# Resident expert weights, and matmuls without a reader in the routing stage of a graph layer

## The chip, the cores and the metric

The kernel runs on one core of one Trainium2 chip. The metric is the device time of one execution in microseconds; the time before is 579.2 us, the median of 3 runs (577.43 to 580.93).

## The reference

One layer on 1250 nodes with 512 features: a layer norm, two graph convolutions (20000 edges) and a linear attention with a two-matrix tail, all added to `x`, then a routed feed-forward on the normed sum. Only the feed-forward matters for the change:

```python
gate_logits = jnp.einsum('bhnd,hde->bhne', xh, gate_weight)      # 1250 tokens x 8 experts
gates = _sinkhorn(gate_logits)                                   # 8 rounds: over tokens, then over experts
vals, idx = jax.lax.top_k(jnp.swapaxes(gates, -1, -2), n // e)   # 156 tokens for each expert
routed = jnp.take_along_axis(xh[:, :, None, :, :], idx[..., None], axis=3)
outputs = jnp.einsum('ebhmi,ehio->ebhmo', routed, expert_w)      # 156x512 @ 512x512, 8 experts
outputs = outputs * gate_values
routed_back = zeros.at[idx].set(outputs)                         # later experts win
x = x + routed_back
```

## The kernel before

Everything is written by hand for each engine, with semaphores between them; each engine's program runs in the order of the code. The 1250 tokens stand as NT = 10 tiles of 125 rows. A float32 matrix product is made of three passes over rounded parts (high by high, low by high, high by low), so a 512x512 product of a tile is 12 matmuls of 512 columns. ScalarE makes the high part of a weight by a copy that rounds (`WEH`), VectorE the low part by a subtraction from the raw weight (`WEL`, `RAW_E`).

The last third of the program, around the change, has three stages.

*Collect.* For each tile `i` TensorE makes the second graph aggregation in 20 matmuls (L789 to L801), VectorE adds it to `X`, makes the norm statistics, and `Y` is the normed tile. SyncE's queue stores `X` to the output and to a DRAM scratch, and `Y` to the scratch (`store_x`, `store_y`). TensorE turns `Y` (`turn_y`, L768) and makes the gate logits (L774).

*Routing.* A chain between VectorE and TensorE with nothing beside it. Eight Sinkhorn rounds: VectorE sums over its tiles (L1453), TensorE sums over the 125 partitions with a matrix of ones (L816), VectorE scales (L1455 to L1459). Ten rounds of a radix search for the 156th largest gate of each expert, 3 bits a round: VectorE compares into `MASK` (L1464, two halves of five tiles), TensorE counts in ten matmuls of 64 columns (L824), VectorE picks the digit (L1468 to L1473). Then ranks (`ranks`, L831 and L832, twice), the slot table (L842), from which VectorE makes the row numbers `idx`, and the gate table (L847).

*Experts.* NS = 16 slots, two for each expert, of 78 tokens each. GpSimd gathers the rows of a slot from the scratch into `YX` (L494, a ring of RING = 12 buffers, 4 KB a row: the normed row and the residual row), TensorE turns the slot (`turn_slot`, L854), ScalarE and VectorE make its high and low part (`FTH`, `FTL`), TensorE multiplies it by the expert in 12 matmuls (L529; the turn of the next slot stands behind the third of them), VectorE scales by the gate and adds the residual (`FO`, L1567), and GpSimd scatters the rows to the output (L503). A gather for slot j + RING is issued behind the scatter of slot j. `FO` has four buffers: slot n waits for the scatter of slot n - 4.

The weights of the experts: four raw buffers (RAWS = 4) and four pairs `WEH`, `WEL`. SyncE loads experts 0 to 3 (1 MB each) before the stores begin, and expert e + 4 when buffer e has been split by both engines. ScalarE splits experts 0 to 3 behind the collect stage and the others between the slots: expert (j + 5) // 2 behind `FTH` of slot j, for odd j, which is a wait in ScalarE's own queue:

```python
if j % 2 == 1 and 4 <= (j + 5) // 2 < NE:
    split_expert((j + 5) // 2)        # waits for fo of slot 2 * (e - 4) + 1 and for the load
```

VectorE makes the low halves of expert j // 2 + 1 (`expert_left`, L1549) behind `FO` of slot j - 1.

Of the kernel before, what the change touches and what calls it, by code (L numbers as in the profile page):

```python
# [51 lines left out]
NS = NE * 2  # L52
RING = 12
RADIX = 3
SHIFTS = list(range(27, -1, -RADIX))
WAYS = 2 ** RADIX
HALF = NT // 2
RAWS = 4
CUTS = (slice(0, 112), slice(112, TT))
# [92 lines left out]
def gps_block(nc, x_in, src_t, dst_t, dst_in, gW1T, gb1, gW2T, gb2, WqT, WkT, Wv, mW1, mW2T,  # L152
# [5 lines left out]
    with ExitStack() as ctx:  # L158
# [56 lines left out]
        YT = at("YT", [128, 2, C, TT + 3], F32, 157.5)  # L215
        YX = at("YX", [128, RING, 2, D], F32, 60)
        FTH = at("FTH", [128, 2, C, SLOT + 2], F32R, 125)
        FTL = at("FTL", [128, 2, C, SLOT + 2], F32R, 128)
        FO = at("FO", [128, 4, D], F32, 52)
        experts_at = [pair(f"WE{s}", [128, C, D], o) for s, o in enumerate((20, 36, 141, 0))]  # L220
        WEH, WEL = [p[0] for p in experts_at], [p[1] for p in experts_at]
        RAW_E = [at(f"RAW_E{s}", [128, C, D], F32, o) for s, o in enumerate((109, 117, 173.5, 181.5))]

# [79 lines left out]
        def view(name, chunks=C):  # L303
# [6 lines left out]
        loads = {n: sem(f"ld_{n}") for n in ("edges", "w1", "w2", "wq", "wv", "b1", "b2", "g1",  # L310
                                             "g2", "gate", "exp0", "exp1", "exp2", "exp3")}
        done = {n: sem(n) for n in (
# [44 lines left out]
        def _(sp):  # L357
# [45 lines left out]
            def load_expert(e):  # L403
                sp.dma_start(RAW_E[e % RAWS][:], rows(experts[e])).then_inc(loads[f"exp{e % RAWS}"], 16)

# [3 lines left out]
            sp.dma_start(gw[:], rows(gate_w[0])).then_inc(loads["gate"], 16)  # L409
            for e in range(RAWS):  # L410
                load_expert(e)
            for i in range(NT):
                store_x(i)
                store_y(i)
            for e in range(RAWS, NE):
                sp.wait_ge(done["exp_hi"], e - RAWS + 1)
                sp.wait_ge(done["el_split"], e - RAWS + 1)
                load_expert(e)
            sp.wait_ge(done["st_out"], 16 * len(CUTS) * NT)
            for s in range(4):  # L420
                sp.wait_ge(scattered[s], 16 * (NS // 4))
# [89 lines left out]
        def _(pe):  # L511
# [269 lines left out]
            def collect(i):  # L781
# [19 lines left out]
                closes(f"o{i}", pe.matmul(ps, AT[0:TT, NT - 1, t], H2L[0:TT, NT - 1, :], start=False, stop=True))  # L801

            for i in range(NT + 2):
                if i < NT:
                    collect(i)
                if 1 <= i <= NT:
                    turn_y(i - 1)
                if i == 2:
                    opens("logits")
                    pe.wait_ge(loads["gate"], 16)  # L810
                if i >= 2:
                    logits(i - 2)

            for r in range(SINKHORN):
                pe.wait_ge(done["p_ready"], r + 1)
                closes(f"sink{r}", pe.matmul(opens(f"sink{r}")[0:TT, 0:NE], ones[0:TT, 0:TT], s8[0:TT, 0, :],  # L816
                                             start=True, stop=True))
            pe.wait_ge(done["rconsts"], 1)
            for r in range(len(SHIFTS)):
                ps = opens(f"rad{r}")  # L820
                for h in range(2):
                    pe.wait_ge(done["ind_ready"], 2 * r + h + 1)
                    for i in range(HALF * h, HALF * (h + 1)):
                        mm = pe.matmul(ps[0:TT, 0:NE * WAYS], ones16[0:TT, 0:TT], MASK[0:TT, i].rearrange("p e c -> p (e c)"),  # L824
                                       start=(i == 0), stop=(i == NT - 1))
                closes(f"rad{r}", mm)

            def ranks(name, sums, marks):
# [5 lines left out]
            pe.wait_ge(done["rank_in"], 1)  # L834
            ranks("rank", before, equal)
            pe.wait_ge(done["order_in"], 1)
            ranks("order", ahead, mine)
            ps = opens("slots")
            for i in range(NT):
                if i % HALF == 0:  # L840
                    pe.wait_ge(done["route_ready"], i // HALF + 1)
                mm = pe.matmul(ps[0:SLOT, 0:NS], RS[0:TT, i, :], PLACE[0:TT, :, :, i], start=(i == 0), stop=(i == NT - 1))  # L842
            closes("slots", mm)
            pe.wait_ge(done["gate_in"], 1)
            ps = opens("gates")
            for i in range(NT):
                mm = pe.matmul(ps[0:SLOT, 0:3 * NS], RS[0:TT, i, :], GATE[0:TT, :, :, :, i], start=(i == 0), stop=(i == NT - 1))  # L847
            closes("gates", mm)

            def turn_slot(j):  # L850
# [6 lines left out]
            def expert(t):  # L857
                e = t // 2
                pe.wait_ge(done["el_split"], e + 1)
                pe.wait_ge(done["ftl_ready"], t + 1)  # L860
                product(f"fo{t}", opens(f"fo{t}")[0:SLOT, :],
                        (lambda c: FTH[:, t % 2, c, 0:SLOT], lambda c: FTL[:, t % 2, c, 0:SLOT]),
                        (rows_of(WEH[e % 4]), rows_of(WEL[e % 4])),
                        between=(lambda: turn_slot(t + 1)) if t + 1 < NS else None, at=3)
# [6 lines left out]
        def _(act):  # L871
# [133 lines left out]
            def copy_yt(i):  # L1005
# [3 lines left out]
                copy(YT[:, i % 2, :, 0:TT], view(f"yt{i}")[:, :, 0:TT]).then_inc(done["yt_ready"], 1)  # L1009

            for i in range(NT + 1):
                if i < NT:
                    act.wait_ge(done["var2_ready"], i + 1)
                    nc.scalar.activation(rstd[0:TT, 1, i:i + 1], mv[0:TT, i, 1:2], ACT.Sqrt,
                                         bias=eps[0:TT, 0:1]).then_inc(done["sqrt2_ready"], 1)
                if i:
                    copy_yt(i - 1)

            def split_expert(e):
                if e == 2:  # L1020
                    act.wait_ge(done["st_scratch"], 2 * 16 * len(CUTS) * NT)
                    act.wait_ge(done["st_out"], 16 * len(CUTS) * NT)
                if e >= 4:
                    reads(act, f"fo{2 * (e - 4) + 1}")
                act.wait_ge(loads[f"exp{e % RAWS}"], 16 * (e // RAWS + 1))
                copy(WEH[e % 4][:], RAW_E[e % RAWS][:]).then_inc(done["exp_hi"], 1)

            for e in range(4):
                split_expert(e)
            for j in range(NS):  # L1030
                reads(act, f"ft{j}")
                if j >= 2:
                    reads(act, f"fo{j - 2}")
                copy(FTH[:, j % 2, :, 0:SLOT], view(f"ft{j}")[:, :, 0:SLOT]).then_inc(done["fth_ready"], 1)
                if j % 2 == 1 and 4 <= (j + 5) // 2 < NE:
                    split_expert((j + 5) // 2)

        @block.vector
        def _(dve):
# [505 lines left out]
            def expert_left(e, n):  # L1545

                after("exp_hi", e + 1)
                half = slice(C // 2 * n, C // 2 * (n + 1))
                ins = V.tensor_tensor(WEL[e % 4][:, half, :], RAW_E[e % RAWS][:, half, :], WEH[e % 4][:, half, :].bitcast(F32),  # L1549
                                      ALU.subtract)  # L1550
# [56 lines left out]
```

## Time and profile before

| | |
|---|---|
| time, median of 3 runs | 579.2 us (577.43 to 580.93) |
| the profiled execution | 581.26 us |
| its span | 579.5 us |
| TensorE busy | 503.5 us (87%) |
| VectorE busy | 350.4 us (60%) |
| ScalarE busy | 132.7 us (23%) |
| GpSimd busy | 75.9 us (13%) |
| mean granted TensorE clock | 0.922 |

The collect stage ends at about 447.7 us of the span, routing runs to 503.7 us, the experts to the end. The profile's rows give busy time, which for TensorE is modelled and pipelined: two matmuls whose starts lie 0.23 us apart are each shown 0.39 us long. The distance of the starts is what a row of matmuls costs. A granted clock of 1.00 is 2.4 GHz, one of 0.50 is 1.2 GHz.

### The profile page before, as it was taken

Reading aid. Unit: us, or ns where it says so; the run is one execution under the profiler, and the core shown is the slowest. Engines: PE = TensorE matmul, PEld = TensorE weight load, DVE = VectorE, ACT = ScalarE, POOL = GpSimd, SP = SyncE. Lnnn points to the kernel's source line nnn. Section 1 sums busy time; section 2 is a strip of 40 time slices with the busy share of each in tenths; the row PEclk is TensorE's granted clock in tenths of the full one; section 3 lists DMA queues with packets and bytes.
Section 4 is the critical chain, followed back from the end, with each engine's and each line's share of the span. In section 5 each row is a group of like instructions: output and inputs, shape, how many; then the busy total and the mean of one; then the engine's idle time right before and its main releaser. Section 6 shows DMA issues by size and latency. Waiting matters only on the chain.

```text
span 579.5 us, 7265 instructions
## 1 busy us (share of the span) xinstructions
PE 503.5 (87%) x2304; PEld 375.9 (65%) x2304; DVE 350.4 (60%) x1010; ACT 132.7 (23%) x259; POOL 75.9 (13%) x83
## 2 busy tenths in 40 slices
PE   6989999798999999998999999999998334377695
PEld 3667888354566776775678999778887334254463
DVE  7865694856877786777864111445455565653573
ACT  4544553111111211113141111221111400011320
POOL 3555001200000000000030000010000000176232
PEclk9979999999799999999999999999999555569799
DMA  8702001200000000000200000009544000099811
GB/s 218 194 1 73 1 17 56 73 1 18 0 1 1 1 0 2 0 2 0 91 2 0 1 2 1 0 6 378 176 125 139 5 0 2 5 223 224 246 49 48
DMA packets 18008, 34.47 MB, mean 59 GB/s; under 512 B 2939, under 2 KB 3269, under 8 KB 17972
## 3 DMA queue, kind: packets, MB, share of 16 engines
q1 hardware_dynamic: 15156, 26.74, 15.1%
q0 software_dynamic: 2816, 7.26, 5.3%
q8 instruction: 22, 0.36, 0.3%
q14 instruction: 14, 0.11, 0.1%
HBM read 24.17 MB, written 10.24 MB: 59 GB/s over the span
## 4 chain that ended last, share of the span: by engine, by line
PE 74%; DVE 13%; issue 5%; DMA 4%; ACT 2%; DVEq 2%; POOLq 0%; ACTq 0%; SPq 0%
PE ps L529 36%; PE ps L789 7%; PE ps L645 7%; PE ps L739 7%; DMA RAW_E<-in_experts 3%; PE ps L824 2%; PE ps L617 2%; PE ps L619 2%; PE ps L618 2%; PE ps L774 1%; DVE HOT_D L1316 1%; DVE HOT_S L1317 1%; PE ps L550 1%; DVEq L1316 1%; DVE MASK L1464 1%
## 5 line engine op out<-in xcount | busy, mean ns | idle before, releaser
L1316 DVE TENSOR_SCALAR HOT_D<-places,key 125x500 bf16<-125x500 f16 x207 | 73.8, 357 | 24.2 <-PE ps L645 21.0
L645 PE MATMUL ps<-HOT_D,HOT_S 125*125 125x500 bf16 x207 | 70.2, 411 | 9.5 <-DVE HOT_S L1317 8.9
L645 PEld LDWEIGHTS ps<-HOT_D,HOT_S 125*125 125x125 bf16 x207 | 28.4, 137 | 47.4 <-DVE HOT_S L1317 38.9
L1317 DVE TENSOR_SCALAR HOT_S<-iota,home 125x128 bf16<-125x128 f16 x207 | 51.6, 250 | 0.1
L739 PE MATMUL ps<-AT,H1H 125*128 125x416 f32 (+1 forms) x108 | 38.1, 353 | 0.0
L739 PE MATMUL ps<-AT,H1L 125*128 125x416 f32 (+1 forms) x108 | 38.0, 351 | 0.0
L789 PE MATMUL ps<-H2H,AT 125*125 125x512 f32 x90 | 36.1, 402 | 0.0
L789 PE MATMUL ps<-H2L,AT 125*125 125x512 f32 x90 | 35.5, 394 | 0.0
L957 ACT ACTIVATE AT<-ps 125x500 fp32r<-125x500 f32 x25 | 14.7, 586 | 82.2 <-PE ps L660 82.2
L494 POOL DMA_INDIRECT YX<-scratch,idx x16 | 16.7, 1042 | 118.8 <-DVE idx L1526 114.2
L446 POOL TENSOR_TENSOR G2L<-RAW_G,G2H 128x512 fp32r<-128x512 f32 x4 | 5.0, 1285 | 189.4 <-ACT G2H L873 189.4
L1379 DVE TENSOR_TENSOR ps<-ps,bias 125x512 f32<-125x512 f32 x20 | 14.0, 699 | 25.7 <-PE ps L529 25.7
L1422 DVE SCALAR_TENSOR_TENSOR ZL<-ps,ZH 128x416 fp32r<-128x416 f32 (+1 forms) x12 | 6.3, 585 | 34.0 <-ACT ZH L1000 34.0
L1567 DVE SCALAR_TENSOR_TENSOR FO<-ps,tokv,YX 78x512 f32<-78x512 f32 x16 | 11.9, 746 | 24.1 <-PE ps L529 15.4
L873 ACT ACTIVATE FTH<-ps 128x312 fp32r<-128x312 f32 x16 | 6.8, 428 | 84.6 <-PE ps L854 84.6
L824 PE MATMUL ps<-MASK,ones 125*125 125x64 bf16 x100 | 12.5, 293 | 15.0 <-DVE MASK L1464 15.0
L503 POOL DMA_INDIRECT out_x<-FO,idx x16 | 18.1, 1132 | 32.0 <-DVE FO L1567 30.8
L529 PE MATMUL ps<-WKH,XTH 128*125 128x512 f32 x40 | 17.8, 444 | 4.8 <-DVE XTL L1099 4.0
L824 PEld LDWEIGHTS ps<-MASK,ones 125*125 125x125 bf16 x100 | 11.4, 225 | 16.0 <-issue 16.0
L739 PEld LDWEIGHTS ps<-AT,H1H 125*128 125x128 f32 x108 | 20.3, 188 | 0.3
L1434 DVE SCALAR_TENSOR_TENSOR X<-ps,X 125x512 f32<-125x512 f32 x10 | 6.9, 692 | 22.5 <-PE ps L801 22.5
L739 PEld LDWEIGHTS ps<-AT,H1L 125*128 125x128 f32 x108 | 20.3, 188 | 0.2
(324 smaller groups left out, 1242.0 us busy)
## 6 DMA issues: line engine op xcount, KB each, us to landing
RAW_E<-in_experts SPq DMA_DIRECT2D x8, 1024.0 KB, 11.7
out_x<-X SPq DMA_DIRECT2D x10, 224.0 KB
scratch<-X SPq DMA_DIRECT2D x10, 224.0 KB
scratch<-Y SPq DMA_DIRECT2D x10, 224.0 KB
X<-in_x SPq DMA_DIRECT2D x4, 448.0 KB
RAW_K<-in_WkT SPq DMA_DIRECT2D x4, 256.0 KB, 4.2
RAW<-in_mW2T SPq DMA_DIRECT2D x1, 1024.0 KB, 13.8
RAW_A<-in_mW SPq DMA_DIRECT2D x1, 1024.0 KB, 14.2
```

Of the source, the lines that this page charges most:

```text
L494: nc.gpsimd.indirect_dma_start(out=YX[0:SLOT, j % RING].rearrange("p a f -> p (a f)"), out_offset=None, in_=scratch, in_offset=bass.Indire ...
L503: nc.gpsimd.indirect_dma_start(out=out, in_=FO[0:SLOT, j % 4, :], in_offset=None, out_offset=bass.IndirectOffsetOnAxis(ap=idx[0:SLOT, 1, c ...
L529: mm = pe.matmul(ps, stationary[a](c), moving[b](c), start=(first and n == 0), stop=(last and n == len(pairs) - 1))
L645: pe.matmul(ps, HOT_S[0:ET, s, 0:TT], HOT_D[0:ET, s, :], start=(opening and s == 0), stop=False, skip_group_check=True).then_inc(hot_used[ ...
L739: pe.matmul(place(f), h[0:TT, k, 128 * f:128 * (f + 1)], AT[0:TT, k, c0:c1], start=(k == 0 and n == 0), stop=False)
L789: pe.matmul(ps, AT[0:TT, k, t], h[0:TT, k, :], start=(k == 0 and n == 0), stop=False)
L824: mm = pe.matmul(ps[0:TT, 0:NE * WAYS], ones16[0:TT, 0:TT], MASK[0:TT, i].rearrange("p e c -> p (e c)"), start=(i == 0), stop=(i == NT - 1))
L957: nc.scalar.activation(AT[0:TT, :, DB * b:DB * (b + 1)], PS[4 + b % 2][0:TT, 0:HOTW].rearrange("p (k d) -> p k d", k=NT), ACT.Copy, accum_ ...
L1316: V.tensor_scalar(HOT_D[0:ET, s, :], places[0:ET, :], key[0:ET, b % 2, bass.ds(col, 1)], None, ALU.is_equal)
L1317: V.tensor_scalar(HOT_S[0:ET, s, :], iota[0:ET, :], home[0:ET, bass.ds(col, 1)], None, ALU.is_equal).then_inc(hot[s], 1)
L1379: V.tensor_tensor(ps, ps, bias[layer - 1][0:TT, :], ALU.add).then_inc(done["h1_biased" if layer == 1 else "h2_biased"], 1)
L1567: V.scalar_tensor_tensor(FO[u, n % 4, :], ps_of(f"fo{n}")[u, :], tokv[u, 1, column(n)], YX[u, n % RING, 1, :], ALU.mult, ALU.add).then_inc ...
```

## The change

Three things are changed together.

All eight experts have a place of their own (`WE0` to `WE7`, 16 KB a partition each); the raw weight lies where the low part will be, which is made in place. Two experts (EARLY = 2) are loaded before the stores, experts 2 to 6 right behind the last store, and expert 7 when all stores have landed. Expert 7's place is that of `X`. ScalarE splits experts 0 and 1 during the collect stage (at tiles 5 and 6) and all others before the first slot. VectorE's instructions are as before.

The ring of gathered slots has 6 buffers in place of 12, and lies where `Y` was.

TensorE gets `keep_clock(n, bank)`: n matmuls of the first 128 columns of `WE0H` with its 512 columns, float32 rounded, into a bank that nobody reads then. 8 stand before the last `turn_y`, 4 behind each of the 8 Sinkhorn sums and of the 10 counts, 5 behind the ranks, 6 behind the order, 7 behind the slot table, 10 behind the gate table: 108 in all.

```diff
-RING = 12
+RING = 6
-RAWS = 4
+EARLY = 2
...
-        YX = at("YX", [128, RING, 2, D], F32, 60)
+        YX = at("YX", [128, RING, 2, D], F32, 137.25)
-        FO = at("FO", [128, 4, D], F32, 52)
-        experts_at = [pair(f"WE{s}", [128, C, D], o) for s, o in enumerate((20, 36, 141, 0))]
+        FO = at("FO", [128, 4, D], F32, 100)
+        experts_at = [pair(f"WE{e}", [128, C, D], o) for e, o in enumerate((109, 173, 20, 36, 52, 68, 84, 0))]
-        RAW_E = [at(f"RAW_E{s}", [128, C, D], F32, o) for s, o in enumerate((109, 117, 173.5, 181.5))]
+        RAW_E = [at(f"RAW_E{e}", [128, C, D], F32, o + 8) for e, o in enumerate((109, 173, 20, 36, 52, 68, 84, 0))]
...
-            for e in range(RAWS):
+            for e in range(EARLY):
                 load_expert(e)
             for i in range(NT):
                 store_x(i)
                 store_y(i)
-            for e in range(RAWS, NE):
-                sp.wait_ge(done["exp_hi"], e - RAWS + 1)
-                sp.wait_ge(done["el_split"], e - RAWS + 1)
+            reads(sp, f"o{NT - 1}")
+            for e in range(EARLY, NE - 1):
                 load_expert(e)
             sp.wait_ge(done["st_out"], 16 * len(CUTS) * NT)
+            sp.wait_ge(done["st_scratch"], 2 * 16 * len(CUTS) * NT)
+            load_expert(NE - 1)
...
+            def keep_clock(n, bank):
+
+                for _ in range(n):
+                    pe.matmul(PS[bank][:], WEH[0][:, 0, 0:128], WEH[0][:, 0, :], start=True, stop=True)
+
             for i in range(NT + 2):
                 if i < NT:
                     collect(i)
+                if i == NT:
+                    pe.wait_ge(done["x_final"], NT - 2)
+                    pe.wait_ge(done["exp_hi"], 1)
+                    keep_clock(8, plan[f"o{NT - 3}"][0])
                 if 1 <= i <= NT:
                     turn_y(i - 1)
...
                 closes(f"sink{r}", pe.matmul(opens(f"sink{r}")[0:TT, 0:NE], ones[0:TT, 0:TT], s8[0:TT, 0, :],
                                              start=True, stop=True))
+                keep_clock(4, plan["order"][0])
...
                 closes(f"rad{r}", mm)
+                keep_clock(4, plan["order"][0])
...
             ranks("rank", before, equal)
+            keep_clock(5, plan["fo1"][0])
...
             ranks("order", ahead, mine)
+            keep_clock(6, plan["fo1"][0])
...
             closes("slots", mm)
+            keep_clock(7, plan["fo1"][0])
...
             closes("gates", mm)
+            keep_clock(10, plan["fo1"][0])
...
             for i in range(NT + 1):
+                if 5 <= i < 5 + EARLY:
+                    split_expert(i - 5)
...
-            for e in range(4):
+            for e in range(EARLY, NE):
                 split_expert(e)
             for j in range(NS):
                 reads(act, f"ft{j}")
                 if j >= 2:
                     reads(act, f"fo{j - 2}")
                 copy(FTH[:, j % 2, :, 0:SLOT], view(f"ft{j}")[:, :, 0:SLOT]).then_inc(done["fth_ready"], 1)
-                if j % 2 == 1 and 4 <= (j + 5) // 2 < NE:
-                    split_expert((j + 5) // 2)
```

TensorE, at the end of the collect stage and the start of routing, before the change. The last two tiles' logits stand behind the turn of the last `Y`, the sums and counts follow with nothing between (`s` are VectorE's sums, `MASK` its comparisons):

```order
L774 MATMUL ps<-gw,YT 125x8 x4
L768 MATMUL ps<-ident,Y 128x125 x4
L774 MATMUL ps<-gw,YT 125x8 x8
L816 MATMUL ps<-s_155,ones 125x8 x8
L824 MATMUL ps<-MASK,ones_157 125x64 x100
```

The same place in the changed kernel, whose lines are numbered otherwise (L807 is `keep_clock`):

```order
L775 MATMUL ps<-gw,YT 125x8 x4
L807 MATMUL ps<-WE0H 128x512 x8
L769 MATMUL ps<-ident,Y 128x125 x4
L775 MATMUL ps<-gw,YT 125x8 x8
L826 MATMUL ps<-s_167,ones 125x8
L807 MATMUL ps<-WE0H 128x512 x4
L826 MATMUL ps<-s_167,ones 125x8
```

Each short matmul of routing now has four long ones behind it, which stand ahead of the next short one in TensorE's order.

ScalarE, from the last logits to the end of the program, before the change (`FTH` is the high part of a turned slot):

```order
L873 ACTIVATE YT<-ps 128x4x125 x2
L873 ACTIVATE WE0H<-RAW_E_113 128x2048
L873 ACTIVATE WE1H<-RAW_E_114 128x2048
L873 ACTIVATE WE2H<-RAW_E_115 128x2048
L873 ACTIVATE WE3H<-RAW_E_116 128x2048
L873 ACTIVATE FTH<-ps 128x4x78 x4
L873 ACTIVATE WE0H<-RAW_E_113 128x2048
L873 ACTIVATE FTH<-ps 128x4x78 x2
L873 ACTIVATE WE1H<-RAW_E_114 128x2048
L873 ACTIVATE FTH<-ps 128x4x78 x2
```

The same stretch after the change; `WE0H` and `WE1H` stand further ahead, among the tiles of the collect stage:

```order
L889 ACTIVATE YT<-ps 128x4x125 x2
L889 ACTIVATE WE2H<-RAW_E_123 128x2048
L889 ACTIVATE WE3H<-RAW_E_124 128x2048
L889 ACTIVATE WE4H<-RAW_E_125 128x2048
L889 ACTIVATE WE5H<-RAW_E_126 128x2048
L889 ACTIVATE WE6H<-RAW_E_127 128x2048
L889 ACTIVATE WE7H<-RAW_E_128 128x2048
L889 ACTIVATE FTH<-ps 128x4x78 x16
```

No split of a weight stands between the slots any longer, so no `FTH` has a load of a weight ahead of it on this engine.

## Rows read from the trace of the kernel before

**Rows 1.** The page's slices: 40 equal parts of the span, tenths.

```profile
PEclk9979999999799999999999999999999555569799
DMA  8702001200000000000200000009544000099811
```

**Rows 2.** Chain that ended last, in order: start, us, what.

```profile
504.67 4.37 DMA YX<-scratch,idx
...
510.95 1.53 PE ps L529 x3
```

**Rows 3.** The same chain, further on.

```profile
518.84 18.79 DMA RAW_E<-in_experts
...
553.38 2.78 PE ps L529 x12
556.16 0.27 PE ps L854 x4
...
568.65 4.86 PE ps L529 x21
```

**Rows 4.** Windows: us, busy of PE, PEld, DVE, ACT, POOL, clock, DMA, GB/s.

```profile
105.00:110.00 5.00, 3.68 (x12) 1.75 (x12) 4.41 (x17) 1.12 (x2) 1.21 (x2) 1.00 0.00 2
...
448.00:449.00 1.00, 1.00 (x11) 1.00 (x9) 0.46 (x6) 0.63 (x2) 0.00 (x0) 0.82 0.52 143
```

**Rows 5.** Timeline up to the Sinkhorn rounds: start, us, what, idle before and its releaser.

```profile
145.57 5.93 PE L645 MATMUL ps<-HOT_D,HOT_S 125*125 125x500 bf16 x12 [2.22 <-DVE HOT_S L1317]
...
433.91 0.30 ACT L1014 ACTIVATE rstd<-mv,eps 125x1 f32<-125x1 f32 x1 [5.17 <-DVE mv L1437]
...
444.36 0.94 PE L774 MATMUL ps<-gw,YT 128*125 128x8 f32 x8
...
447.69 0.65 PE L768 MATMUL ps<-ident,Y 125*128 125x125 f32 x4 [2.39 <-DVE Y L1441]
...
448.17 2.92 PE L774 MATMUL ps<-gw,YT 128*125 128x8 f32 x16
...
454.05 0.59 PE L816 MATMUL ps<-s,ones 125*125 125x8 f32 x2 [1.71 <-DVE s L1453]
```

**Rows 6.** Timeline of a radix round, and of TensorE's later pauses.

```profile
472.41 0.89 DVE L1464 TENSOR_TENSOR MASK<-P,THR 125x320 bf16<-125x320 f32 x2
...
473.05 1.25 PE L824 MATMUL ps<-MASK,ones 125*125 125x64 bf16 x10 [1.45 <-DVE MASK L1464]
...
499.64 0.33 PE L831 MATMUL ps<-ahead,ones 125*125 125x80 bf16 x1 [1.60 <-DVE ahead L1482]
...
502.21 0.89 PE L842 MATMUL ps<-PLACE,RS 125*78 125x16 f16 x10 [2.13 <-DVE RS L1514]
...
509.09 0.78 PE L854 MATMUL ps<-ident,YX 78*128 78x78 f32 x4 [2.48 <-DMA YX<-scratch,idx]
```

**Rows 7.** Timeline of the experts: matmuls at either clock, `FO`, a split.

```profile
514.51 0.63 PE L529 MATMUL ps<-WE0L,FTH 128*78 128x512 f32 x1
...
514.94 0.63 PE L529 MATMUL ps<-WE0H,FTL 128*78 128x512 f32 x1
...
517.46 0.44 PE L854 MATMUL ps<-ident,YX 78*128 78x78 f32 x4
...
537.07 0.75 DVE L1567 SCALAR_TENSOR_TENSOR FO<-ps,tokv,YX 78x512 f32<-78x512 f32 x1 [8.68 <-DMA out_x<-FO,idx]
...
537.72 1.91 ACT L873 ACTIVATE WE1H<-RAW_E 128x2048 fp32r<-128x2048 f32 x1 [10.20 <-DMA RAW_E<-in_experts]
```

**Rows 8.** Issue to landing of `RAW_E`, then of `YX`, min, median, max.

```profile
DMA to landing us min/median/max: 5.6/11.7/21.2
...
DMA to landing us min/median/max: 4.4/14.1/16.3
```

**Rows 9.** The gathers issued from 506 to 509 us, the same view.

```profile
DMA to landing us min/median/max: 5.3/5.7/6.2
```

**Rows 10.** The page's groups: the scatters, their number, busy us, mean ns, idle before.

```profile
L503 POOL DMA_INDIRECT out_x<-FO,idx x16 | 18.1, 1132 | 32.0 <-DVE FO L1567 30.8
```

More of the change, by code:

```diff
@@ L310, in gps_block @@
         loads = {n: sem(f"ld_{n}") for n in ("edges", "w1", "w2", "wq", "wv", "b1", "b2", "g1",
-                                             "g2", "gate", "exp0", "exp1", "exp2", "exp3")}
+                                             "g2", "gate", *(f"exp{e}" for e in range(NE)))}
         done = {n: sem(n) for n in (
@@ L403, in load_expert @@
             def load_expert(e):
-                sp.dma_start(RAW_E[e % RAWS][:], rows(experts[e])).then_inc(loads[f"exp{e % RAWS}"], 16)
+                sp.dma_start(RAW_E[e][:], rows(experts[e])).then_inc(loads[f"exp{e}"], 16)
             reads(sp, f"h2_{NT - 1}")
@@ L862, in expert @@
                         (lambda c: FTH[:, t % 2, c, 0:SLOT], lambda c: FTL[:, t % 2, c, 0:SLOT]),
-                        (rows_of(WEH[e % 4]), rows_of(WEL[e % 4])),
+                        (rows_of(WEH[e]), rows_of(WEL[e])),
                         between=(lambda: turn_slot(t + 1)) if t + 1 < NS else None, at=3)
@@ L1009, in copy_yt, with split_expert @@
                 copy(YT[:, i % 2, :, 0:TT], view(f"yt{i}")[:, :, 0:TT]).then_inc(done["yt_ready"], 1)
+            def split_expert(e):
+                act.wait_ge(loads[f"exp{e}"], 16)
+                copy(WEH[e][:], RAW_E[e][:]).then_inc(done["exp_hi"], 1)
             for i in range(NT + 1):
+                if 5 <= i < 5 + EARLY:
+                    split_expert(i - 5)
                 if i < NT:
@@ L1017, in _ @@
                     copy_yt(i - 1)
[L1019 to L1026, printed above, removed]
-            for e in range(4):
+            for e in range(EARLY, NE):
                 split_expert(e)
@@ L1548, in expert_left @@
                 half = slice(C // 2 * n, C // 2 * (n + 1))
-                ins = V.tensor_tensor(WEL[e % 4][:, half, :], RAW_E[e % RAWS][:, half, :], WEH[e % 4][:, half, :].bitcast(F32),
+                ins = V.tensor_tensor(WEL[e][:, half, :], RAW_E[e][:, half, :], WEH[e][:, half, :].bitcast(F32),
                                       ALU.subtract)
```

## The prediction

> **What bounds the kernel now.** I read the slices first. The granted clock falls from full to half at the end of the collect stage, stays there through routing and dips once more among the experts; the DMA row is empty through most of routing and full over the first half of the experts [rows 1]. So two things stand at this place: TensorE's short matmuls of routing run at 1.2 GHz, and transfers that could have been made in an idle stretch are made when the gathers need the engines. The change speaks to both.
>
> The chain that ended last gives the prices. Routing is a ladder of VectorE and TensorE, then the first gather takes 4.37 us, and the first product of the experts starts at 510.95 [rows 2]. From there to the end of the last product (568.65 + 4.86 = 573.51) are 62.56 us. In that stretch the chain has one wait of 18.79 us for `RAW_E`, while a slot that waits for nothing takes 2.78 us of products and 0.27 of turns, 3.05 us [rows 3]. The timeline shows two queues behind it: `FO` waited 8.68 us for a scatter, and a split of a weight 10.20 us for its load, with `FTH` of the next slot behind it on ScalarE [rows 7]. A load of 1 MB took up to 21.2 us and a gather 14.1 in the median, against 4.4 for the first one, which was alone [rows 8].
>
> **The change part by part.**
>
> *Expert stage.* Six loads go from the experts into routing and its edge. Loads 2 to 7 leave from about 448.5 on, when the last `Y` is stored. One behind another they are in by 448.5 + 6 x 5.6 = 482 at the shortest landing, and by 519 at the median of 11.7 [rows 8]. ScalarE has all six splits (1.91 us each [rows 7]) ahead of the first `FTH`, which is due at 509.5; at the slow end it would be 11 us late. The median comes from loads in flight together and beside gathers, and here the engines are empty [rows 1], so I take the fast end and 0. Splits 0 and 1 stand in ScalarE pauses of 5.17 us between tiles [rows 5], so 1.91 is hidden there; without that cover each would delay one `Y` by 1.91 us, and `Y` is needed only a tile later. VectorE's work is the same. What remains is TensorE's own: 15 x 3.05 + 2.78 = 48.5 us for 62.56, which is -14.0. The second gather took between 5.3 and 6.2 us [rows 9], from 506.13, and is wanted at 510.6 + 0.7: I add 0.4 for a wait. Term: **-13.6**. VectorE, with the same instructions a slot, kept that pace of 3.05 from 553 on [rows 3].
>
> *Ring of 6.* A gather for slot j + 6 leaves behind the scatter of slot j, about 2.4 us after its product (0.75 for `FO`, 1.13 for the scatter's issue [rows 10], the rest for semaphores), and is wanted 4 x 3.05 + 0.7 = 12.9 us after that product. It may take 10.5 us. Gathers beside each other and one load took 6.2 at most [rows 9]; with all loads in flight 14.1 [rows 8]. The loads are gone, so I take 0; the bound is 0.9 us for each of ten slots. The Trainium skill, DMA: Bandwidth & Descriptors, Issuing engines are not separate DMA queues, says that transfers of all issuing engines run on the same 16 DMA engines and interleave; the trace agrees, with a gather of 4.4 us alone and 14.1 beside loads.
>
> *The clock.* 16 logit matmuls took 2.92 us, of which the last part at half clock; eight at full took 0.94 [rows 5]. Term 2 x 0.94 - 2.92 = -1.0. A Sinkhorn pair took 0.59 at half [rows 5]. No row has it at full; the nearest is the logit matmul with the same 8 columns, 0.118 us apiece in a row of eight against 0.18, which makes 0.34 to 0.59 for the pair. I take 0.37, near the low end, since it is the same operation: 8 x -0.22 = -1.8, at worst 0. A count of ten matmuls took 1.25 us at half [rows 6]. At full it can't be shorter than the wait for the second half of `MASK`, which ends 0.89 after its start while the count starts at 0.64; between 0.6 and 1.25, and by the same ratio of 0.6 nearest to 0.8. 10 x -0.45 = -4.5. The two rank steps give -0.2, the turn of slot 0 0.44 for 0.78 [rows 6, 7], -0.35. The products of slot 0 at half (0.43 a matmul against 0.23) are in the 62.56 already. Term: **-7.8**.
>
> *The added matmuls.* 512 columns at full clock are one each 0.23 us (2.78 for 12), at half 0.43 [rows 3, 7]. At full, four are 0.92 us and stand in pauses of 1.71 and 1.45 that are VectorE's; five are 1.15 in 1.60, six 1.38 in 2.13, ten 2.30 in 2.48 plus the 0.4 by which the gate table ends sooner, and the eight before the last `Y` 1.84 in 2.39, less than its whole because the logits of tile 8 are already done [rows 5, 6]. Queued behind them on TensorE are only the matmuls that wait for VectorE anyway. Term: 0, if the clock is full.
>
> Whether it is full is the open part. With a clock of 1.00 TensorE once started 12 matmuls of 500 columns in 5 us with VectorE between them [rows 4]. The new rounds have four of 512 columns and a short pair in about 2.07 us, some 10 in 5 us, with pauses of about 0.8 us. The clock was lost in the slice that begins at 144.9, where TensorE had a pause of 2.22 us [rows 1, 5], and between 448 and 449, after a pause of 2.39 and with matmuls of 8 columns [rows 4, 5]. The pauses that remain are far shorter, so I take 1.00; but no row of before has this mix of long and short matmuls, and for that the rival below keeps a real chance.
>
> The Trainium skill, TensorE: Matmul & The Clock Gate, Why this matters for your kernels, asks for no long idle gaps between bursts. By that rule alone the clock is safe here and the sum the one below; the fall between 448 and 449, with TensorE back at work on 8-column matmuls, is a case that it doesn't cover. The chance below follows the rows.
>
> **Sum.** -13.6 - 7.8 = -21.4. The profiled execution took 581.26 us with a span of 579.5 and lies 2.1 above the median; its span would be 558.1, and against the median of 579.2 the time is **557.8 us**.
>
> **The rivals.**
>
> *The clock doesn't hold (0.22).* Then the added matmuls are 0.43 us each and fill or overfill the pauses: 4 x 0.43 = 1.72 against 1.71 and 1.45, so 0.1 in the Sinkhorn rounds and 2.7 in the counts; five 0.5, six 0.5, seven about 0.6 (their pause taken as that of the tens'), ten 4.3 against 2.48, 1.8: 6.2 in all. Nothing of the 7.8 comes, and the first slot costs 2.6 more than 3.05. 579.2 - 13.6 + 6.2 + 2.6 = 574.4. If it is lost for part of routing only, between: 563 to 570. For it: pauses in every round, in a mix that no row has. Against: they are 0.8 us, and those before the falls 2.2 and 2.4.
>
> *The gather takes the place of the load (0.08).* At the 14.1 us of now, a slot becomes (14.1 + 1.7) / 4 = 3.95, ten of them +9.0: 566.8. For it: the same DMA engines carry 320 KB of gather and 160 KB of scatter a slot. Against: the loads are what filled them.
>
> *The ring makes it slower (0.03).* The same mechanism decides the sign from a landing of 18.9 us on: (18.9 + 1.7) / 4 = 5.15 a slot, 2.1 x 10 = 21, which eats the gain. At 20 us it is 582. Nothing but `RAW_E` has taken that long; the slowest gather took 16.3 [rows 8].
>
> *The loads don't fill routing (0.02).* If TensorE still waited for a weight as now, only the clock would pay: 571.4.
>
> **How the numbers follow.** The forecast has 0.65 and by its own terms reaches from 554 (counts at the 0.6 bound, the pair at 0.34) to 563 (half of the clock's terms, and 1.3 more of waits at the first slots). The range has to take in the gather case and the clock lost in part; it ends at 570, with about 0.15 above it and 0.04 below 554. The late `FTH` (557.8 + 11 = 569) lies within. A measurement of this kernel tells about 0.5% from no change; the sum is 3.7%. Slower only by the ring beyond 19 us, 0.03; the same 0.02; faster 0.95.
>
> **What would show it.** In the profile after: a granted clock near 1.00 from 447 to the end, and mean clock 0.97 or more; the counts 0.8 us instead of 1.25 with the same pauses less the added matmuls; no `RAW_E` in the chain, its landings all before 485; a gather of 7 us or less; slots 3.05 us apart, 49 us from first to last product. Wrong would be: half clock in a slice of routing, TensorE named as the releaser of itself ahead of a sum or count, `YX` as what TensorE waits for from slot 6 on.

## The result

The changed kernel takes **558.5 us** (median of 4 runs, 557.36 to 560.33) against 578.9 (4 runs, 577.43 to 580.93). The ratio is 0.965, with a 95% interval of 0.961 to 0.969: 20.4 us saved, where the forecast was 557.8 us. The profiled execution took 557.36 us, its span is 555.6 and its mean granted clock 0.983, for 0.922 before.

The profile after: TensorE's busy time, the two rows that answer to [rows 1], and the group of the added matmuls.

```profile
PE 519.2 (93%) x2412; PEld 383.4 (69%) x2412; DVE 350.1 (63%) x1010; ACT 133.0 (24%) x259; POOL 75.1 (14%) x83
...
PEclk9999999999899999999999999999999987999999
DMA  8702001100000000000020000001843494015541
...
L807 PE MATMUL ps<-WE0H 128*128 128x512 f32 x108 | 34.6, 453 | 0.0
```

The DMA row is now at 9 and 4 where routing begins (444 to 472 us), and at 5, 5 and 4 among the experts, where it had 9, 9 and 8 before. The clock row has an 8 and a 7 left in routing, for the four slices at half of before. TensorE is busier than before in a shorter time, by matmuls that nobody reads.

The chain that ended last, the part that answers to [rows 2] and [rows 3] (start, us, what):

```profile
494.71 4.26 DMA YX<-scratch,idx
...
500.59 0.90 PE ps L530 x3
...
501.98 2.78 PE ps L530 x12
504.76 0.27 PE ps L870 x4
505.03 2.78 PE ps L530 x12
...
544.71 4.86 PE ps L530 x21
```

No wait is left in it from the first product to the last: 500.59 to 549.57 is 48.98 us, for 62.56 before. The slots stand 3.05 us apart. The only wait that the profile shows in this stretch is one of 0.5 us, for the gather of slot 1. Transfers in the changed kernel, issue to landing (minimum, median, maximum), first `RAW_E`, then `YX`; they answer to [rows 8]:

```profile
DMA to landing us min/median/max: 5.6/9.3/14.1
...
DMA to landing us min/median/max: 3.8/4.2/6.0
```

A stage by stage comparison of the two profiled executions, in us, worked out from starts in their timelines. It begins at the start of the last turn of `Y`, because that start itself lies 3.3 us earlier in this profile of the changed kernel (444.40 for 447.69). Over the profiles of this study it varies from 443.6 to 447.8, whether the kernel has the change or not: it is 443.89 in a variant of the kernel before (the smaller reordering below). So these 3.3 us are not counted for the change. The first Sinkhorn sum is VectorE's, and the end of the last product is the start of the last row of the chain plus its length.

| stage | before | after | difference | forecast |
|---|---|---|---|---|
| last turn of `Y` and logits, to the first Sinkhorn sum | 3.71 | 2.69 | -1.02 | -1.0 |
| Sinkhorn, to the first `MASK` | 18.32 | 17.46 | -0.86 | -1.8 |
| counts, to the ranks | 26.68 | 22.09 | -4.59 | -4.5 |
| ranks and slot table, to the first gather's issue | 8.27 | 8.07 | -0.20 | -0.2 |
| first gather and turn of slot 0, to the first product | 6.28 | 5.88 | -0.40 | -0.35 |
| first product to the end of the last | 62.56 | 48.98 | -13.58 | -13.6 |
| sum with the end | 131.8 | 111.2 | -20.6 | -21.4 |

### The profile page after: what moved, and what is told of

Its sections match the earlier page's. It is cut to its first block, busy times and chain, and to the rows that moved or that the text cites. A ratio compares the mean times of both kernels' runs of the same rounds, so it can differ in the third digit from the quotient of the medians.

```text
span 555.6 us, 7474 instructions
## 1 busy us (share of the span) xinstructions
PE 519.2 (93%) x2412; PEld 383.4 (69%) x2412; DVE 350.1 (63%) x1010; ACT 133.0 (24%) x259; POOL 75.1 (14%) x83
## 4 chain that ended last, share of the span: by engine, by line
PE 77%; DVE 12%; issue 4%; ACT 2%; DVEq 2%; POOL 1%; DMA 1%; POOLq 0%
PE ps L530 37%; PE ps L790 8%; PE ps L646 8%; PE ps L740 7%; PE ps L618 2%; PE ps L620 2%; PE ps L619 2%; DVE HOT_S L1328 1%; PE ps L835 1%; DVE HOT_D L1327 1%; PE ps L807 1%; PE ps L775 1%; PE ps L551 1%; DVEq L1327 1%; POOL W1L L447 1%
## 5 line engine op out<-in xcount | busy, mean ns | idle before, releaser
L807 PE MATMUL ps<-WE0H 128*128 128x512 f32 x108 | 34.6, 453 | 0.0
L807 PEld LDWEIGHTS ps<-WE0H 128*128 128x128 f32 x108 | 21.1, 214 | 3.2
L740 PEld LDWEIGHTS ps<-AT,H1H 125*128 125x128 f32 x108 | 20.3, 188 | 0.3
L740 PEld LDWEIGHTS ps<-AT,H1L 125*128 125x128 f32 x108 | 20.3, 188 | 0.2
L504 POOL DMA_INDIRECT out_x<-FO,idx x16 | 16.9, 1055 | 18.9 <-DVE FO L1578 11.9
## 6 DMA issues: line engine op xcount, KB each, us to landing
X<-in_x SPq DMA_DIRECT2D x4, 448.0 KB
```

Source lines behind the costliest of these rows:

```text
L504: nc.gpsimd.indirect_dma_start(out=out, in_=FO[0:SLOT, j % 4, :], in_offset=None, out_offset=bass.IndirectOffsetOnAxis(ap=idx[0:SLOT, 1, c ...
L740: pe.matmul(place(f), h[0:TT, k, 128 * f:128 * (f + 1)], AT[0:TT, k, c0:c1], start=(k == 0 and n == 0), stop=False)
L807: pe.matmul(PS[bank][:], WEH[0][:, 0, 0:128], WEH[0][:, 0, :], start=True, stop=True)
```

## The experiments

Ten kernels were run. Theory A says that the 13.6 us of the expert stage come from the loads being out of the way of the gathers and scatters, by two separate means: A1, the places (no load waits for a used buffer), and A2, the traffic (no load beside a gather). Theory B says that the other 7 to 8 us come from the granted clock, and that the added matmuls themselves cost nothing. The rivals: one part does all of it, a smaller reordering would do the same, or the ring decides.

### Each part alone

**Without the added matmuls.** The changed kernel with an empty `keep_clock`:

```diff
             def keep_clock(n, bank):
-                for _ in range(n):
+                for _ in range(0):
```

> The changed kernel without any of the 108 added matmuls; the resident experts and the ring of 6 stay. Theory A (two gains that add up: the weights' wait 13.6, the clock 7): the first slot runs at half clock again, 2.7 us, so the expert stage is 51 us instead of 62.6, and nothing else changes: 568 us, ratio to before 0.981. Theory B (most of the gain is the clock, since a faster TensorE also ends the wait for the weights): 573 to 577.

Measured: 567.6 us (4 runs) for 579.5 of before (7 runs), ratio 0.979 (0.976 to 0.983). The clock is at half for 68.3 us from 445.6 on, as before, and the expert stage takes 50.34 us. So the places, loads and ring together bring 12.0 us, with the clock of before; this run does not tell the three apart. In its chain (start, us, what) the first slot is still slow:

```profile
510.37 1.53 PE ps L530 x3
...
512.42 3.48 PE ps L530 x12
```

12 products took 3.48 us where 2.78 are usual, after which the clock had come back. Over the whole stage the start at half clock costs 50.34 - 48.98 = 1.4 us, not the 2.6 that the prediction gave it in a rival. So 12.2 of the 13.58 us of the expert stage come without the added matmuls, and 1.4 through the clock.

**The added matmuls alone.** Before, with the same 108 matmuls at the same places; the eight ahead of the last `turn_y` use another weight tile, since `WE0H` is not ready there:

```diff
+                if i == NT:
+                    pe.wait_ge(done["x_final"], NT - 2)
+                    for _ in range(8):
+                        pe.matmul(PS[plan[f"o{NT - 3}"][0]][:], AT[0:TT, 0, 0:128], AT[0:TT, 0, 0:512], start=True, stop=True)
...
+                pe.wait_ge(done["exp_hi"], 1)
+                keep_clock(4, plan["order"][0])
...
+                keep_clock(4, plan["order"][0])
```

> The kernel before with the 108 matmuls and nothing else (the first eight use the adjacency tile, since the first expert isn't split yet there). Theory A: routing is 4.5 us shorter in the counts, 0.9 in the Sinkhorn rounds, 1.0 in the logits, 0.4 in the turn; the first slots run at full clock but then wait that much longer for the weights and scatters, so nothing more: 572 us, ratio 0.988. Theory B: the added matmuls alone bring 12 or more: 567 or less. The sum of the gains of this run and of the one without them should be near 20.

Measured: 571.2 us in the same company, ratio 0.987 (0.984 to 0.990). That is 8.3 us, and 12.0 + 8.3 = 20.3 is what both together bring: the parts add, within the noise of the two. The expert stage is 61.37 us long, with its old waits. The waits of its expert stage (engine, tile and line, what it waited for: us, times, longest):

```profile
DVE FO L1583 <- DMA out_x<-FO,idx: 10.4, 2, 9.6
...
ACT WE1H L889 <- DMA RAW_E<-in_experts: 4.5, 1, 4.5
```

### What the expert stage's gain is made of

**A smaller reordering.** Before, with each split one odd slot later, so that `FTH` of the next slot does not stand behind the wait for a load:

```diff
-                if j % 2 == 1 and 4 <= (j + 5) // 2 < NE:
-                    split_expert((j + 5) // 2)
+                if j % 2 == 1 and 4 <= (j + 3) // 2 < NE:
+                    split_expert((j + 3) // 2)
```

> The kernel before with one edit: ScalarE splits experts 4 to 7 two slots later, so that the wait for a load stands ahead of the high part of slots 6, 8, 10, 12 instead of 4, 6, 8, 10. If this wait in ScalarE's queue is what the chain shows as 18.8 us of load, most of it goes: 570. If the late scatter of slot 0 (15.8 us, for which VectorE waited 8.7 us) binds as long, little goes: 576 to 579.

Measured: 577.6 us (10 runs) for 578.8 (13 runs), ratio 0.998 (0.994 to 1.002): no change that can be told. Its waits in the expert stage:

```profile
DVE FO L1567 <- DMA out_x<-FO,idx: 9.7, 2, 8.9
PEld ps L529 <- DVE WE3L L1549: 7.9, 1, 7.9
```

The wait moved out of ScalarE's queue and came back as `FO` waiting for its scatter and TensorE waiting for a low half. Putting this wait elsewhere in the queue did not help while the transfers were late.

**Late loads in places of their own.** The changed kernel, but experts 4 to 7 are loaded when `idx` is ready, and split between the slots as before:

```diff
-            for e in range(EARLY, NE - 1):
+            for e in range(EARLY, 4):
+                load_expert(e)
+            sp.wait_ge(done["idx_ready"], 1)
+            for e in range(4, NE - 1):
                 load_expert(e)
...
-            for e in range(EARLY, NE):
+            for e in range(EARLY, 4):
                 split_expert(e)
...
+                if j % 2 == 1 and 4 <= (j + 5) // 2 < NE:
+                    split_expert((j + 5) // 2)
```

> The changed kernel, but experts 4 to 7 are loaded only when the row numbers are there, beside the first gathers, and split by ScalarE between the slots as before the change; all eight keep a place of their own. Theory A1 (what cost was that a load could only leave when a buffer had been split, so the later ones left at 519, 525 and 539): now all four leave at 494 and land before 515, and nothing waits: 559 or 560. Theory A2 (the traffic beside the gathers is what costs, by late scatters and gathers): most of the 13.6 us returns, 568 to 572.

Measured: 568.4 us (564.86 to 570.48), ratio 0.980 (0.974 to 0.985), about 10 us worse than the changed kernel in their medians. The largest piece stands ahead of the first slot, in the timeline of TensorE (start, us, what, idle before and its releaser):

```profile
502.72 1.78 PE L810 MATMUL ps<-WE0H 128*128 128x512 f32 x7
509.49 0.78 PE L873 MATMUL ps<-ident,YX 78*128 78x78 f32 x4 [4.98 <-DMA YX<-scratch,idx]
511.35 0.69 PE L533 MATMUL ps<-WE0H,FTH 128*78 128x512 f32 x1 [1.08 <-issue]
```

The first gather, beside four loads of 1 MB that left with it, took 9.2 us where it takes 4.3 alone, TensorE stood idle for 5 us, and with it went the clock (the turn at 0.78 and not 0.49 us), so the stage that follows is 51.34 long. From the issue of the first gather to the end of the last product that makes 7.6 us more than in the changed kernel: 4.9 in the gather, 0.3 in the turn, 2.4 in the stage. Another 1.4 us in this profile are a loss of the clock in the counts, before any of the late loads left. No split waited for its late load and no slot waited after the first. Neither theory had it so: the same 4 MB of experts 4 to 7 cost 18.8 us of waiting before [rows 3], where each load had to wait for a used buffer and twelve gathers were issued in a row, and about 5 us and a lost clock when they left together beside six gathers.

**Traffic that nobody waits for.** The changed kernel, with eight loads of 512 KB into spare places, two in flight, from the gate table on:

```diff
+            sp.wait_ge(done["gate_ready"], 1)
+            for n in range(8):
+                if n >= 2:
+                    sp.wait_ge(extra[n % 2], 16 * (n // 2))
+                sp.dma_start(SPARE[n % 2][:], rows(experts[n])[:, 0:2, :]).then_inc(extra[n % 2], 16)
```

> The changed kernel with 4 MB of further loads (eight of 512 KB, two in flight at a time) into parts of SBUF that nobody reads, from the end of routing on; nothing waits for them but the end. It takes the bandwidth of the loads of before without their dependencies. If traffic beside the gathers costs by itself, gathers and scatters land later than 10 us and the slots wait: 563 or more. If it was the order of load and split, the gathers take 6 to 9 us, below the 10.5 that a ring of 6 allows, and the time is 559.

Measured: 563.8 us for 578.8, ratio 0.973 (0.966 to 0.981), some 5 us over the changed kernel. The two intervals overlap, so the lengths of the stage decide: 55.22 us for 48.98. Its gathers, issue to landing:

```profile
DMA to landing us min/median/max: 4.1/10.9/11.1
```

The two waits for a gather that its chain names (start, us, what):

```profile
497.39 7.94 DMA YX<-scratch,idx
...
527.84 11.35 DMA YX<-scratch,idx
```

4 MB of loads beside the gathers make these 10.9 us long for 4.2, which is about 1 us more than a ring of 6 allows (9.9, below). Most of the loss is not there, but at the second gather, for which TensorE waited in the middle of slot 0 (its timeline):

```profile
505.37 0.78 PE L880 MATMUL ps<-ident,YX 78*128 78x78 f32 x4 [2.95 <-DMA YX<-scratch,idx]
```

Of the 6.2 us that the stage is longer, 2.95 are this wait, 1.3 are two later waits for a gather (1.08 and 0.26), and 1.5 are the turn and nine matmuls at half clock behind the first wait (0.78 + 3.29 us for 0.49 + 2.08). So traffic alone costs 6 us here, without any wait for a weight, most of it by one late gather at the start, as in the run before this one. That engines share the 16 DMA engines whatever queue issued (the Trainium skill, DMA: Bandwidth & Descriptors, Issuing engines are not separate DMA queues) agrees with both runs; the lengths 9.2 and 10.9 for 4.2 are theirs.

### The ring

**Four buffers**, then **three**:

```diff
-RING = 6
+RING = 4
```

> The changed kernel with a ring of 4 gathered slots. A gather for slot j + 4 is then due 2 x 3.05 + 0.7 = 6.8 us after the product of slot j and leaves 2.4 after it: it may take 4.4 us, and the trace shows 3.8 to 4.4. No wait or a few tenths: 558.5 to 560.

> The changed kernel with a ring of 3. By the rule of the prediction a slot becomes (landing + 1.7) / (ring - 2) = 4.1 + 1.7 = 5.8 us instead of 3.05, for 13 slots: 36 us more, 594, slower than the kernel before. If the gather is served from elsewhere than this loop of scatter and gather (the rule is wrong), the loss is under 20 us.

Measured: with four 564.7 us (564.46 to 565.37), ratio 0.975 (0.968 to 0.982), a stage of 53.59; with three 594.6 us, ratio 1.027 (1.019 to 1.035), a stage of 85.27. Four was expected to cost at most 1.5 us and cost 4.6 in the stage. GpSimd's timeline of the kernel with four buffers shows why:

```profile
508.95 1.00 POOL L504 DMA_INDIRECT out_x<-FO,idx  x1 [5.59 <-DVE FO L1578]
510.26 0.97 POOL L495 DMA_INDIRECT YX<-scratch,idx  x1 [0.31 <-issue]
512.28 0.98 POOL L504 DMA_INDIRECT out_x<-FO,idx  x1 [1.05 <-issue]
513.56 2.47 POOL L495 DMA_INDIRECT YX<-scratch,idx  x1 [0.30 <-issue]
516.34 0.98 POOL L504 DMA_INDIRECT out_x<-FO,idx  x1 [0.30 <-issue]
```

`FO`, which follows its product, started at 507.21 and the gather left at 510.26, 3.05 us later where the prediction had 2.4 (in the changed kernel it is 3.05 as well), and the next gather's issue took 2.47 us where 0.97 is usual. With three buffers the whole landing is on the path. A piece of its chain (start, us, what), one round:

```profile
518.73 3.79 DMA YX<-scratch,idx
...
528.86 1.09 POOL out_x L504
...
530.26 4.13 DMA YX<-scratch,idx
```

(85.27 - 48.98) / 13 gathers = 2.79 us each, for the 2.75 that the prediction's rule gives. The match is in part luck. TensorE's waits for a gather in this stage (us, times, longest), then the windows of the expert stage with three buffers and of the changed kernel (columns as in [rows 4]):

```profile
PE ps L870 <- DMA YX<-scratch,idx: 22.1, 7, 3.5
...
501.25:586.52 85.27, 63.14 (x252) 38.86 (x252) 33.74 (x44) 6.50 (x15) 28.57 (x28) 0.82 0.25 73
...
500.59:549.57 48.98, 48.96 (x252) 31.98 (x252) 33.02 (x44) 6.48 (x15) 28.38 (x27) 1.00 0.46 127
```

TensorE waited seven times for sixteen slots, so in every second slot and not in each, as the rule (landing + 1.7) / (ring - 2) has it. These waits are 22.1 us, 1.7 for each of the 13 gathers. The other 14.2 of the 36.3 us are the same 252 matmuls at a mean clock of 0.82: the clock fell in the pauses. A shorter ring does cost, and the landing on the path is the cause; the size of 2.75 is not borne out. Without the lost clock the time would be 594.6 - 14.2 = 580.4 us, an estimate from these rows, which can't be told from the kernel before (578.8). So what turned the sign was the ring and the clock that fell in its pauses, together.

**What a ring of 12 did before.** The kernel before issues twelve gathers before its first scatter, the changed one six. GpSimd's timelines, the last gather and first scatter before, then after:

```profile
519.90 0.94 POOL L494 DMA_INDIRECT YX<-scratch,idx  x1 [0.30 <-issue]
521.15 1.60 POOL L503 DMA_INDIRECT out_x<-FO,idx  x1 [0.30 <-issue]
...
505.83 1.00 POOL L504 DMA_INDIRECT out_x<-FO,idx  x1 [2.14 <-DVE FO L1578]
```

Before, `FO` of slot 0 was done at 517.64 and its scatter stood 3.5 us behind gathers in GpSimd's queue, to land 15.8 us after its issue; after, GpSimd waited for `FO`. With the added matmuls alone the chain that ended last runs through the issues of all twelve gathers, from 495.32 to 515.46, and then through that scatter (11.8 us). So a shorter ring may be a gain of its own, and part of the 12.2 us. No run has the kernel before with a ring of 6: this rival is open.

### The clock

**Six in place of four** behind each Sinkhorn sum, and then also **three behind the last logits**:

```diff
+            keep_clock(3, plan["order"][0])
...
-                keep_clock(4, plan["order"][0])
+                keep_clock(6, plan["order"][0])
```

> The changed kernel with 6 instead of 4 added matmuls behind each Sinkhorn sum. The trace shows the clock lost twice in these rounds with four. If four were too thin, six keep it at 1.00 through all eight rounds, each 2.08 us instead of up to 2.31: 557.6, 1 us less. If the clock is lost for another reason (the pause before the first sum, the logits of 8 columns), one loss stays and rounds at half clock now wait for 6 x 0.43 = 2.6 us of added matmuls: 0.9 us more in each such round, 560.

> As the changed kernel with 6 added matmuls behind each Sinkhorn sum, and 3 more behind the last logits, in the pause of 0.66 us ahead of the first sum (3 x 0.23 = 0.69, at most a tenth late). In the runs so far the clock was lost 2 to 5 us after the last logits in every version with added matmuls, so the logits of 8 columns are the suspect. If so, the clock stays at 1.00 from the collect stage to the end, the Sinkhorn stage is 8 x 2.08 = 16.7 us instead of 17.5, and the time 557.7, 0.8 below the changed kernel. If not, a loss at the same place, and rounds of 2.5 us in it: 559.5.

Measured: the first 559.4 us (556.88 to 560.21), ratio 0.965 (0.961 to 0.968), no different from the changed kernel; the second 557.2 us (5 runs, 556.87 to 558.08), ratio 0.961 (0.959 to 0.963), whose interval overlaps that of the changed kernel. Each lost the clock once and not twice. Windows of the second (us, busy of PE, PEld, DVE, ACT, POOL, clock, DMA, GB/s):

```profile
448.00:449.00 1.00, 1.00 (x6) 0.64 (x6) 0.56 (x2) 0.00 (x0) 0.00 (x0) 1.00 0.82 211
449.00:450.00 1.00, 1.00 (x4) 0.82 (x4) 0.82 (x4) 0.00 (x0) 0.00 (x0) 0.57 0.98 377
450.00:451.00 1.00, 1.00 (x4) 0.71 (x3) 0.62 (x3) 0.00 (x0) 0.00 (x0) 0.50 0.95 352
```

TensorE had no idle time in these windows and lost the clock all the same, 3 us after the start of the 16 logit matmuls of 8 columns. So the three behind the logits did not prevent it, and nothing that was tried did.

Without the eight matmuls at the last `Y` the clock falls sooner. In three of the four kernels without them it fell in the pause ahead of the last turn, before these logits (in the fourth, the kernel before, at 448.6, behind the turn). The kernel without any added matmuls, TensorE and a window:

```profile
446.46 1.07 PE L769 MATMUL ps<-ident,Y 125*128 125x125 f32 x4 [2.59 <-DVE Y L1452]
...
445.00:446.00 1.00, 0.00 (x0) 0.00 (x0) 0.89 (x4) 0.16 (x1) 0.00 (x0) 0.78 0.87 283
```

So there are falls in a pause of 2.4 to 2.6 us, which the eight matmuls remove, and falls a few us behind the logits, which no added matmul removed.

**Only from the counts on**: neither the eight at the last `Y` nor those in Sinkhorn, 68 matmuls from the first count on, so that they begin at half clock.

```diff
-                    keep_clock(8, plan[f"o{NT - 3}"][0])
...
-                keep_clock(4, plan["order"][0])
```

> The changed kernel without the 8 matmuls ahead of the last turn and without the 32 in the Sinkhorn rounds; the 68 from the counts on stay. The counts begin at half clock with added matmuls of 0.43 us. If the clock returns under them, after two or three rounds, the counts take 23.2 instead of 22.1, the Sinkhorn rounds 18.3 instead of 17.5 and the logits 1 more: 561.5. If it stays at half, which the prediction's first rival takes, each count round is 2.9 to 3.0 us: 566 or more.

Measured: 563.7 us (4 runs), ratio 0.972 (0.969 to 0.975), between the two expectations. TensorE's timeline in the count rounds:

```profile
470.53 1.21 PE L833 MATMUL ps<-MASK,ones 125*125 125x64 bf16 x10
471.55 2.06 PE L807 MATMUL ps<-WE0H 128*128 128x512 f32 x4
...
482.45 1.17 PE L807 MATMUL ps<-WE0H 128*128 128x512 f32 x4
484.06 0.79 PE L833 MATMUL ps<-MASK,ones 125*125 125x64 bf16 x10 [0.45 <-DVE MASK L1473]
```

At half clock the four fill the pause and more: rounds of 2.88 us (467.62, 470.53, 473.41, and so on), for 2.69 before and 2.24 at full. TensorE was shown without a pause from 468 on, and the clock came back at about 481, after five rounds. So it does come back by the added matmuls, and a kernel that had lost it at the counts would have paid 0.2 us a round for as long.

## Why the prediction was right, and where it was not

**The expert stage** was sized to 0.1: 13.58 for 13.6. The reason is that the prediction took TensorE's own work as the bound, 15 x 3.05 + 2.78, and 0.4 for the second gather, and no other wait came. Its step that loads 2 to 7 are in early held by much: SyncE issued the last at 450.76 and the last split began at 464.66, 33 us ahead of its use. (Only four of these six loads came from the experts; 2 and 3 stood before the stores.) What made the old waits go was not told apart by the prediction, and the runs do it only in part: places without a wait, engines without loads when gathers run, and a ring that puts six and not twelve gathers ahead of the first scatter. With late loads in places of their own it is 568.4, with other loads beside the gathers 563.8, and with a reordering alone nothing.

**The ring at no price** was right, with less room than stated. The step that a gather leaves about 2.4 us after the product was mis-sized: it is 3.05 in the changed kernel and in the one with four buffers, and now and then GpSimd's issue is slower. A ring of 6 then allows about 9.9 us, not 10.5. The gathers take 4.2 in the median and 6.0 at most, so nothing of it showed. The rule behind the rivals' prices, which divides by the ring less 2, charges each slot with a wait; the kernel with three buffers waited in every second one. And the prediction looked at the smaller ring only as a risk, not as a possible gain.

**The clock's terms** for logits, counts, ranks and the turn of slot 0 came as worked out in the profiled execution. (For slot 0 the turn is 0.49 us for 0.78; the other 0.1 of its row is a gather of 4.26 for 4.37.) A count of ten takes 0.79 us and the pause behind it shrank from 1.45 to what the added four leave. The timeline of the changed kernel, TensorE:

```profile
467.43 0.79 PE L835 MATMUL ps<-MASK,ones 125*125 125x64 bf16 x10 [0.45 <-DVE MASK L1475]
468.05 1.17 PE L807 MATMUL ps<-WE0H 128*128 128x512 f32 x4
```

**The Sinkhorn term** was mis-sized, -0.86 for -1.8. The step that failed is "the pauses that remain are far shorter, so I take 1.00": the clock was at half from 448.0 to 451.4 and from 458.2 to 465.0. Two of the signs that the prediction named as wrong are there, a half clock in slices of routing, and sums that stand right behind the added matmuls with no idle time. A window of the changed kernel (columns as in [rows 4]):

```profile
448.00:449.00 1.00, 1.00 (x4) 0.66 (x2) 0.86 (x5) 0.00 (x0) 0.00 (x0) 0.50 1.00 381
```

And its timeline in Sinkhorn, sums at half and at full clock:

```profile
449.52 0.59 PE L826 MATMUL ps<-s,ones 125*125 125x8 f32 x2
449.96 1.81 PE L807 MATMUL ps<-WE0H 128*128 128x512 f32 x4
...
453.92 0.38 PE L826 MATMUL ps<-s,ones 125*125 125x8 f32 x2 [0.68 <-DVE s L1464]
...
460.31 0.59 PE L826 MATMUL ps<-s,ones 125*125 125x8 f32 x2
460.75 2.06 PE L807 MATMUL ps<-WE0H 128*128 128x512 f32 x4
```

That it cost only 1 us is the prediction's own bound: at half clock four take 1.72 us and the pause is 1.71, so such a round takes 2.3 us, as before the change, and no more. The rival "the clock doesn't hold" was right for 10 of the 17.5 us of Sinkhorn, and cheap there; in the counts, where it would have cost, the clock held in this profile. The Trainium skill, TensorE: Matmul & The Clock Gate, Why this matters for your kernels, asks for no long idle gaps. The prediction had said that the rule does not cover matmuls of 8 columns, and yet it gave 1.00 to rounds that begin with them. By the rule none of the kernels with added matmuls would have lost the clock in Sinkhorn, where the longest pauses before a fall are 0.66 to 0.69 us; the measurement decides.

The counts are not safe from it either, and that the counts' term was met is in part luck. In the profiles of five variants with the same filler (the added matmuls alone, late loads, traffic, four and three buffers) a loss reached into them, and they took 23.2 to 24.4 us for 22.1. The other executions of the changed kernel, with mean clocks of 0.973 to 0.980 and 558.3 to 560.3 us, for 0.983 and 557.4 of the profiled one, would fit that, or a dip in the stages before; they left no trace.

**The low end of the forecast's own terms**, 554, is not what they give: 557.8 less 10 x 0.2 for the counts and 8 x 0.03 for the pairs is 555.6. Nothing measured lies there.

**Its price for a half clock at the first slot**, 2.6 us, was too high; the kernel without the added matmuls shows 1.4. This stood in a rival alone.

**What stays open.** What would prevent the first loss. In the eight kernels that fill routing from the last `Y` on, it falls 2.2 to 3.9 us after the start of the logit matmuls; that these 8-column matmuls cause it is argued from this, and not shown, since the one attempt at a cure left them in place. A second loss came, in Sinkhorn or the counts, in all six of them with four matmuls behind a Sinkhorn sum, and in neither of the two with six; two profiles are few for that, and the times don't tell the difference. The shares of places, traffic and ring in the 12.2 us are open too. The late loads bring back 7.6 us and the traffic 6.2, both mainly by a late gather at the start and the clock lost in its pause, which is not the wait of before; and the ring of 6 was in both. That waiting for a used buffer cost by itself is argued from the chain before, and not shown; the kernel before with a ring of 6 would be the next run.

## What to carry to other kernels

When memory allows, give late weights places of their own and load them in a stretch in which the DMA row is empty; here the loads that waited for a used buffer landed beside the gathers, and moving that wait in the queue gave it only another name. When several parts are changed together, run each alone, also the one that was taken for a price. Where TensorE alternates with another engine on short matmuls, compare the pause with the filler at both clocks: the filler was worth 8 us here. Where it just filled the pause at half clock, in Sinkhorn, it cost nothing when the clock fell; where it overfilled it, in the counts, it cost 0.2 us a round. Size a ring by the measured distance from product to the next gather's issue, with the landing under load and not alone.

## What the runs showed of the hardware

- TensorE's granted clock fell from 2.4 to 1.2 GHz with TensorE shown busy without a pause, behind matmuls of 8 columns (449.1 us in the last Sinkhorn kernel). It was back after 3.4 us in both kernels with rounds of six of 512 columns, after 3.4 and 6.8 us in the changed kernel, and took some 13 us from the first count in rounds of ten of 64 and four of 512 columns that began at half.
- The first gather of 78 rows of 4 KB, with no load beside it, takes 4.2 to 4.5 us; in the changed kernel the sixteen take 3.8 to 6.0. The first took 9.2 with four loads of 1 MB beside it, and the median is 10.9 beside loads of 512 KB.
- GpSimd's issue of a gather is mostly 0.97 us long, and was 2.47 and 2.03 in the kernel with four buffers, where issues followed one another with 0.3 us between them.
- With three buffers the clock fell in or right behind pauses of 2.8 to 3.5 us inside the products, and the same 252 matmuls took 63.1 us of busy time for 49.0.
